# A Mamba layer before attention and experts: x_proj in two 64-column tiles, delta in two row groups, chunk ends in four 32-column tiles, carries on VectorE

## The reference, cut to what matters

```python
dbc = einsum('ble,re->blr', xb, xp_w)              # 512 channels -> 48 rows
delta, Bm, Cm = dbc[..., :16], dbc[..., 16:32], dbc[..., 32:]
delta = softplus(einsum('blr,er->ble', delta, dtw) + dtb)   # rank 16 -> 512 channels
dA = exp(delta[..., None] * -exp(a_log))           # 512 channels x 16 states
mi = delta[..., None] * Bm[:, :, None, :] * xb[..., None]
def scan_fn(carry, inp):
    h, v = carry
    dA_t, mi_t, C_t = inp
    v = 0.6 * v + mi_t                             # fixed decay
    h = dA_t * h + v                               # decay from the data
    return (h, v), einsum('ben,bn->be', h, C_t)
```

## Time and profile before

| | |
|---|---|
| median of three runs | 1678.77 us |
| the profiled execution: its own time | 1679.95 us |
| its span, first to last instruction | 1678.4 us |
| TensorE busy | 1533.2 us (91%) |
| VectorE busy | 1188.1 us (71%) |
| GpSimd busy | 1002.5 us (60%) |
| ScalarE busy | 826.3 us (49%) |

### The profile page before, as it was taken

One profiled execution on the slowest core, in us unless ns is written; L12 is line 12 of the kernel. 1 busy time (PEld: TensorE's weight loads), 2 busy tenths in 40 slices (PEclk: granted clock), 3 DMA queues, 4 the chain that ended last, 5 costly groups with the idle time before them and its releaser, 6 DMA issues.

```text
span 1678.4 us, 23940 instructions
## 1 busy us (share of the span) xinstructions
PE 1533.2 (91%) x8930; PEld 1159.4 (69%) x8930; DVE 1188.1 (71%) x1910; ACT 826.3 (49%) x1175; POOL 1002.5 (60%) x820
## 2 busy tenths in 40 slices
PE   4689999999999999999999997858979898899997
PEld 2468878978978978978879897623434443476776
DVE  3389979879879879879879879447666672433344
ACT  3756556656656656556556543203545556411110
POOL 1469778978978969969969987653111100024441
PEclk9899999999999999999999999968999999999999
DMA  4100100101100100100101120146141400612124
GB/s 139 42 26 27 51 26 27 51 26 52 51 26 27 51 26 27 51 26 27 51 26 41 74 87 14 36 91 138 22 92 21 81 1 1 258 38 64 63 67 166
DMA packets 38113, 92.78 MB, mean 55 GB/s; under 512 B 9136, under 2 KB 21936, under 8 KB 33520
## 3 DMA queue, kind: packets, MB, share of 16 engines
q1 hardware_dynamic: 29392, 73.68, 13.9%
q0 software_dynamic: 7584, 16.53, 3.8%
q10 hardware_dynamic: 1024, 1.05, 0.3%
HBM read 64.88 MB, written 9.57 MB: 44 GB/s over the span
## 4 chain that ended last, share of the span: by engine, by line
PE 76%; DVE 13%; issue 4%; ACT 3%; POOL 1%; SPq 1%; DMA 1%; DVEq 0%; ACTq 0%; POOLq 0%
PE psum L483 23%; PE psum L464 10%; PE psum L420 5%; PE psum L1495 4%; PE psum L1480 4%; DVE uw L512 4%; DVE hst L606 4%; PE psum L1064 4%; PE psum L1046 2%; PE psum L444 2%; PE psum L455 2%; PE psum L1030 2%; PE psum L426 2%; PE psum L434 2%; ACT pT L1119 2%
## 5 line engine op out<-in xcount | busy, mean ns | idle before, releaser
L774 POOL TENSOR_TENSOR hst<-hst,cb 128x512 f32<-128x512 f32 x399 | 512.8, 1308 | 136.1 <-DVE hst L606 135.0
L606 DVE TENSOR_TENSOR_SCAN hst<-dA,hst,psum 128x256 f32<-128x256 f32 x399 | 277.0, 729 | 84.5 <-PE psum L483 82.3
L606 DVE TENSOR_TENSOR_SCAN hst<-dA,psum 128x256 f32<-128x256 f32 x399 | 252.8, 668 | 38.8 <-ACT dA L716 19.7
L483 PE MATMUL psum<-filt,uT 128*128 128x172 f32 (+1 forms) x1536 | 267.9, 311 | 10.7 <-DVE hst L606 9.1
L483 PE MATMUL psum<-filt,c_early 128*128 128x172 f32 (+1 forms) x1536 | 268.1, 311 | 7.9 <-DVE hst L606 5.6
L483 PEld LDWEIGHTS psum<-filt,c_early 128*128 128x128 f32 x1536 | 235.2, 192 | 47.6 <-issue 27.3
L483 PEld LDWEIGHTS psum<-filt,uT 128*128 128x128 f32 x1536 | 233.5, 191 | 40.9 <-issue 19.8
L716 ACT ACTIVATE dA<-delta,alog 128x512 f32<-128x512 f32 x256 | 176.9, 721 | 150.3 <-DVE hst L606 120.2
L464 PE MATMUL psum<-ident,hst 128*128 128x128 f32 x1596 | 240.3, 274 | 0.7 <-POOL hst L774 0.6
L716 ACT ACTIVATE dA<-xres,alog 128x512 f32<-128x512 f32 x256 | 177.1, 720 | 123.5 <-DVE hst L606 97.4
L1191 DVE TENSOR_REDUCE nmax<-psum 128x2 f32<-128x1024 f32 x128 | 154.8, 1221 | 82.9 <-PE psum L1030 82.6
(11 more groups left out here) (213 smaller groups left out, 2346.3 us busy)
## 6 DMA issues: line engine op xcount, KB each, us to landing
cb<-c_rows SPq DMA_DIRECT2D x32, 1024.0 KB, 4.7
qk<-part SPq DMA_DIRECT2D x120, 64.0 KB, 2.4
qk<-part POOLq DMA_DIRECT2D x72, 64.0 KB, 4.5
w_up<-up_dram SPq DMA_DIRECT2D x8, 512.0 KB, 7.8
w_down<-down_dram SPq DMA_DIRECT2D x8, 512.0 KB, 14.3
w_up<-y_choice SPq DMA_DIRECT2D x8, 512.0 KB, 8.1
xm<-x_dram SPq DMA_DIRECT2D x4, 512.0 KB, 10.0
w_early<-w_in_dram SPq DMA_DIRECT2D x2, 1024.0 KB, 5.8
```

The source lines that it names most:

```text
L483: m = pe.matmul(bk[:, :, t0:t0 + width], uT[k % 2][:, c, et * P:(et + 1) * P], filt[:, f % 2, c, n2:n2 + 2, 0:width], start=True, stop=True)
L606: dve.tensor_tensor_scan(h[:, t0:t0 + HS], dA[:, st % NDA, t0:t0 + HS], bank("v", i)[:, n * HS:(n + 1) * HS], h[:, t0 - 1:t0] if t0 else 0 ...
L774: pool.tensor_tensor(h, h, cb[:, q % 2, state_of(i)[1] % GN, :], ALU.mult).then_inc(g_done, 1)
```

## The change

- **x_proj**: the weights' 48 rows become 64 (delta, B, delta again, C) and the 512 tokens two halves of 256. Each half goes to its own 64-column tile of the array: output partitions 0 to 63 and 64 to 127 of one bank, 256 columns each. ScalarE takes them out with two copies of 64 x 256 in place of one of 128 x 512.
- **delta**: contraction over 32 rows (16 of them zero weights) in place of 128; even `d` pieces use rows 0 to 31, odd ones rows 32 to 63. In the plan `d` 0 and 1 both stand at step 23, `d` 2 and 3 at step 25.
- **dbcT** transposes 32 rows in place of 48.
- **bend / bcol** (VectorE): the two `bend` multiplications now read `dbcT` from PSUM and stand ahead of `bcol`, which frees the bank; before they read `bcol` from SBUF behind it. `bend` has 32 columns per chunk in place of 128, and zeros in the rows of the starting state.
- **chunk ends**: no `c` waits for another. Chunks 0 to 3 go to four 32-column tiles of one bank, chunk 4 to another bank; both pieces stand at step 53. ScalarE's copies stand at step 54 (four) and 55 (one); each waits for both pieces.
- **carries** (new, VectorE): four `scalar_tensor_tensor` of 16 x 512, `uT[j+1] += 0.6**width * uT[j]` for j = 1 to 4, at steps 56 to 59. The first v matmul of a pass waits for the last of them.

```diff
-                    put(23 + m, "pe", "d", m)
+                    put(23 + m // 2 * 2, "pe", "d", m)
...
-                for c in range(NCH - 1):
-                    put(52 + 2 * c, "pe", "c", c)
-                    put(53 + 2 * c, "act", "c", c)
+                for q in range(2):
+                    put(53, "pe", "c", q)
+                for c in range(NCH - 1):
+                    put(54 + c // NQ, "act", "c", c)
+                for c in range(1, NCH - 1):
+                    put(55 + c, "dve", "carry", c)
...
                     for kt in range(ET):
-                        i = pe.matmul(bk, w_xp[:, l, kt, :], xbs[:, par, kt, NSTATE:NSTATE + S], start=kt == 0, stop=kt == ET - 1)
+                        for h in range(2):
+                            i = pe.matmul(bk[XP_ROWS * h:XP_ROWS * (h + 1), 0:HS], w_xp[:, l, kt, :],
+                                          xbs[:, par, kt, NSTATE + h * HS:NSTATE + (h + 1) * HS],
+                                          start=kt == 0, stop=kt == ET - 1, tile_position=(0, XP_ROWS * h))
...
-                    i = pe.matmul(bk, w_dt[:, l, j * P:(j + 1) * P], dbc[:, NSTATE:NSTATE + S], start=True, stop=True)
+                    r0 = j % 2 * BC
+                    i = pe.matmul(bk, w_dt[r0:r0 + BC, l, j * P:(j + 1) * P], dbc[r0:r0 + BC, NSTATE:NSTATE + S], start=True, stop=True,
+                                  tile_position=(r0, 0))
...
-                    pe.wait_ge(bank_act, emptied_by("act", k, "c", j - 1) if j else emptied_by("act", k, "u", NCH - 1))
-                    i = pe.matmul(bk, bend[:, j, :], uT[par][:, j, :], start=True, stop=True)
+                    pe.wait_ge(bank_act, emptied_by("act", k, "u", NCH - 1))
+                    w = P // NQ
+                    for c in range(j * NQ, min(j * NQ + NQ, NCH - 1)):
+                        p0 = c % NQ * w
+                        i = pe.matmul(bk[p0:p0 + w, :], bend[:, c, :], uT[par][:, c, :], start=True, stop=True, tile_position=(0, p0))
...
+                    dve.tensor_scalar(ends[:, :, 0:HCH - 1], starts[:, :, 0:HCH - 1], keep[:, 1:2], None, ALU.mult)
+                    dve.tensor_scalar(ends[:, :, HCH - 1], starts[:, :, HCH - 1], keep[:, 2:3], None, ALU.mult).then_inc(bend_done, 1)
                     dve.scalar_tensor_tensor(out=bcol[:, par], in0=tv[:, :, RANK:RANK + NSTATE], scalar=keep[:, 0:1], in1=carry_id[:].unsqueeze(1).to_broadcast([P, NCH, NSTATE]),
                                              op0=ALU.mult, op1=ALU.add).then_inc(bank_dve, 1)
...
+                elif what == "carry":
+                    if j < NQ - 1:
+                        dve.wait_ge(ends_out, (NQ - 1) * k + j + 1)
+                    else:
+                        dve.wait_ge(bank_act, emptied_by("act", k, "c", j // NQ))
+                    if j > 1:
+                        dve.wait_ge(carry_done, NQ * k + j - 1)
+                    to = uT[par][0:NSTATE, j + 1, :]
+                    dve.scalar_tensor_tensor(out=to, in0=uT[par][0:NSTATE, j, :], scalar=BETA ** CHUNKS[j][1], in1=to,
+                                             op0=ALU.mult, op1=ALU.add).then_inc(carry_done, 1)
...
-                    act.copy(dbc[:, NSTATE:NSTATE + S], bank(k, "xp", 0)).then_inc(bank_act, 1)
+                    act.copy(dbc[:, NSTATE:NSTATE + HS], bank(k, "xp", 0)[0:XP_ROWS, 0:HS])
+                    act.copy(dbc[:, NSTATE + HS:NSTATE + S], bank(k, "xp", 0)[XP_ROWS:2 * XP_ROWS, 0:HS]).then_inc(bank_act, 1)
```

More of the change, by code:

```diff
@@ L27 @@
 RANK = 16
-RBC = RANK + 2 * NSTATE
+BC = RANK + NSTATE
+C_ROW = 2 * RANK + NSTATE
+XP_ROWS = C_ROW + NSTATE
 L = 2
@@ L261, in plan_first @@
                     put("act", "u", c)
+                for q in range(2):
+                    put("pe", "c", q)
+                s += 1
                 for c in range(NCH - 1):
-                    s += 1
-                    put("pe", "c", c)
-                    s += 1
                     put("act", "c", c)
+                for c in range(1, NCH - 1):
+                    put("dve", "carry", c)
             def plan_front(k, at, start):
@@ L519, in dve_side @@
                         dve.wait_ge(filt_done, NG * (k - 1))
-                    tv = bank(k, "dbcT", 0)[:, 0:NCH * RBC].rearrange("p (j r) -> p j r", r=RBC)
+                    tv = bank(k, "dbcT", 0)[:, 0:NCH * BC].rearrange("p (j r) -> p j r", r=BC)
+                    ends = bend[:, :, 0:NSTATE].rearrange("p (h c) n -> p h c n", h=2)
+                    starts = tv[:, :, RANK:RANK + NSTATE].rearrange("p (h c) n -> p h c n", h=2)
+                    dve.tensor_scalar(ends[:, :, 0:HCH - 1], starts[:, :, 0:HCH - 1], keep[:, 1:2], None, ALU.mult)
+                    dve.tensor_scalar(ends[:, :, HCH - 1], starts[:, :, HCH - 1], keep[:, 2:3], None, ALU.mult).then_inc(bend_done, 1)
                     dve.scalar_tensor_tensor(out=bcol[:, par], in0=tv[:, :, RANK:RANK + NSTATE], scalar=keep[:, 0:1], in1=carry_id[:].unsqueeze(1).to_broadcast([P, NCH, NSTATE]),
                                              op0=ALU.mult, op1=ALU.add).then_inc(bank_dve, 1)
-                    dve.wait_ge(bank_dve, emptied_by("dve", k, "dbcT", 0))
-                    ends = bend[:, :, 0:NSTATE].rearrange("p (h c) n -> p h c n", h=2)
-                    starts = bcol[:, par].rearrange("p (h c) n -> p h c n", h=2)
-                    wide, last = CHUNKS[0][1], CHUNKS[HCH - 1][1]
-                    dve.tensor_scalar(ends[:, :, 0:HCH - 1], starts[:, :, 0:HCH - 1], toep[:, wide - 1:wide], None, ALU.mult)
-                    dve.tensor_scalar(ends[:, :, HCH - 1], starts[:, :, HCH - 1], toep[:, last - 1:last], None, ALU.mult).then_inc(bend_done, 1)
+                elif what == "carry":
[8 more added lines that the diff above has]
+                                             op0=ALU.mult, op1=ALU.add).then_inc(carry_done, 1)
                 elif what == "clip":
@@ L700, in act_side @@
                 elif what == "c":
-                    act.wait_ge(bank_full, filled(k, "c", j))
-                    act.copy(uT[par][0:NSTATE, j + 1, :], bank(k, "c", j)[0:NSTATE, :]).then_inc(bank_act, 1)
+                    act.wait_ge(bank_full, filled(k, "c", 1))
+                    p0 = j % NQ * (P // NQ)
+                    act.copy(uT[par][0:NSTATE, j + 1, :], bank(k, "c", j // NQ)[p0:p0 + NSTATE, :]).then_inc(
+                        bank_act if j in (NQ - 1, NCH - 2) else ends_out, 1)
                 elif what == "x_roots":
```

30 lines of the change are left out of this document (17 added, 13 removed).

## The result

The changed kernel takes 1683.19 us (1677.56 to 1689.35, median of 20 runs) against 1677.68 us (1672.12 to 1682.26, 20 runs) for the one before: ratio 1.0031, interval 1.0020 to 1.0043. It is slightly slower, by 0.3%. The forecast of 1671.5 us was 11.7 us too low, and on the other side of no change. The change itself was missed by 12.8 us: 7.3 faster was forecast from a median before of 1678.77, and 5.5 slower was measured against 1677.68.

What follows compares the result with a forecast made beforehand. TensorE sets the pace, VectorE the end from step 3 to 8. 1679.95 - 6.5 (front) - 7 x (1.57 + 0.64) (x_proj, delta) + 14.2 (carries) = 1672.2; with the median 1.2 lower, forecast 1671.5 us, range 1651 to 1686.

Steps and rivals of the forecast that it cites:

- TensorE sets the pace, but from v 52 to v 9 VectorE does: Mamba loop: TensorE busy 131.13 of 132.00 us; VectorE sets the end around steps 3 to 8 of a pass.
- x_proj: Step 20, seven times: column tiles run side by side, 1.86 us for 3.43, 1.57 us saved each.
- delta: Steps 23 and 25: pairs of 1.0 us for 1.73; a wait for bcol leaves 0.64 us saved per pass.
- Carries: Steps 56 to 59: four VectorE instructions, some waiting for GpSimd's running one, take 5.5 us; 1.95 us lost per pass.
- The 1.95 is carried to step 9 and into the pass: Steps 3 to 9: order as before and VectorE bound, so the 1.95 us loss reaches the pass.
- Steady passes: x_proj and delta save, carries lose 1.95 us: a pass takes about 123.8 us for 124.06.
- Pass 0's front: Start of pass 0, up to the first scan: 6.5 us saved, 4 to 8, first scan at about 66.6.
- Each carry meets GpSimd in full & d saves nothing: Slower rival: carries cost 1.5 us more a transition and the delta pairs save nothing; 1685 us, chance 0.08.
- the clock rival: TensorE's clock falls in new waits at steps 62, 63 and 0, costing 23 us; 1695 us, chance 0.10.
- Tiles in turn: x_proj's tiles save nothing and the five c hold VectorE 2.4 us longer; 1699 us, chance 0.03.
- Half rate: Carries run at half throughput, 0.5 us more each, 2 a transition; 1685 us, chance 0.02.
- Carries are cheap: Carries don't wait for GpSimd, 0.7 us each, 2.8 in all; 1652 us, chance 0.12.

Runs made afterwards that it cites:

- nocarry: The changed kernel with the four carries left out, the first v of a pass waiting for the last copy: 1650.83 us, ratio .9834, pass 120.9 us.
- nox: The changed kernel with x_proj on one 64-column tile over all 512 tokens and one copy: 1697.02 us, ratio 1.0114, pass 127.0 us.
- twice_sbuf: psum53 plus four more scalar_tensor_tensor with both operands in SBUF, into a tile nobody reads: 1710.08 us, ratio 1.0203.
- second profile: The changed kernel run again without any edit: profiled total 1684.74 us, median 1683.73 us, ratio 1.0025.
- psum53: The changed kernel with carries reading the chunk end from PSUM, all four behind step 53's scans, ScalarE copying only the first end: 1657.68 us, ratio .9874.

## Why the prediction was wrong, step by step

- **TensorE sets the pace, but from v 52 to v 9 VectorE does: right with the carries.** Without them (nocarry) all that TensorE saves there is gained. The carries alone make VectorE the bound.
- **x_proj: right in kind, a little mis-sized.** 1.55 saved in its own bracket where 1.57 was forecast, but 0.19 goes in the pieces around it: 1.36. nox shows by itself that the tiles run side by side (1.70 against one tile after the other).
- **delta: mis-sized.** 0.64 was forecast, 0.24 measured. The wait for `bcol` came where it was put, 0.54 us instead of 0.9. What was missing is the way into and out of a tiled piece, 0.09 ahead of it and 0.10 behind. A pair costs 1.25 in all (0.09 + 1.06 + 0.10), not 1.0. Of the 0.40 missing here, 0.10 belongs to `xp`, whose longer v 21 falls into this stretch.
- **Carries: the failed step.** "Carries 1 and 2 each meet a running multiplication (1.8 each)": the walk was right up to the first carry (8.21 us behind step 53's v; 8.3 forecast), and the sum of the four was 6.6 instead of 5.5. The mechanism had the wrong reach. The first carry waited for the running multiplication and for two more that were ready when it came, and took 3.29; in twice_sbuf, with three more ready, the first took 5.06. Carries 2 and 4 met a running one alone (1.33, 1.32), and carry 3 none, for want of more ready work. The prediction had taken its rule from the maxima, which do wait for the running instruction alone, and a carry is not treated as they are. Of the 1.1 us more, 0.67 shows in the stretch (2.62 lost for 1.95); the walk's 0.3 for small waits and the air behind took the rest, which I did not follow further.
- **"The 1.95 is carried to step 9 and into the pass": too little.** Another 0.3 goes at step 11, where `bo` waits for GpSimd's gate, which ran 0.8 us later (and 0.09 ahead of `xp`). The prediction looked at GpSimd's sum (14% idle) and not at what it owes there.
- **Steady passes:** -2.21 + 1.95 = 123.8 forecast, -1.79 + 2.62 + 0.40 = 125.3 measured. Five of them are 7.5 of the 12.8 us by which the change was missed.
- **Pass 0's front: right in itself, mis-sized at the end.** 7.1 us at the first scan for 6.5, but 2.6 to 5.0 by the next `xp`: TensorE works there at a granted clock of 0.86 to 0.93 (before 0.96), so part of what is saved goes again. The forecast let all 6.5 reach the end. A shorter front does not by itself bring the lower clock: nocarry has 0.96 from 65 to 110 with its first scan at 67.66. What does was not tried.
- **The sum by stretches**, change against the kernel before, in us:

| | forecast | first profile | second profile |
|---|---|---|---|
| start to `xp` in pass 0 | -6.5 | -5.1 | -2.6 |
| to `xp` in pass 1 | +1.2 | -1.3 | +1.3 |
| five steady passes | -1.3 | +6.2 | +6.2 |
| rest | -1.2 | -1.1 | -0.3 |
| all | -7.8 | -1.2 | +4.6 |

The largest error stands in the steady passes. In the second row the forecast paid 5.5 us for the carries; they took 4.0 (0.67, 1.33, 0.65, 1.33).
- **The rivals.** "Each carry meets GpSimd in full & d saves nothing", 1685 us at a chance of 0.08, is nearest to what happened in time. In kind it is half right, and the closeness is partly luck: the carries took 6.6 us and not the 7.0 it means, the `d` save a little, and pass 0 gives back less than the forecast that it started from. Clock at steady passes 1.00: the clock rival is out. Tiles in turn: out by nox. Half rate: 0.65 us for 512 elements in carry 3 (0.7 was the forecast's full rate), out. "Carries are cheap" became true as a mechanism in psum53, not in this kernel.

## What to carry to other kernels

A VectorE instruction with both inputs in SBUF, put beside a GpSimd that has ready work, can cost far more than its own length: here the rest of the running instruction at least, and for the 16-partition carries everything that was ready when they came. Do not carry the price over from another kind of instruction; take one operand from PSUM where it already lies there, and drop the copy with it. In a ring of banks look up for each moved piece which piece stands a ring's length ahead: a wait that is moved away from one piece goes to the next, and may hide in its duration. An engine with 14% idle over the pass can still be the last one at one step. Price a tiled piece with the pieces on both sides of it, not by its own bracket.

## What the hardware showed that was not expected

- A 16x512 `scalar_tensor_tensor` with both inputs in SBUF takes 0.65 to 0.68 us alone, 3.29 beside one running and two ready GpSimd instructions, and 5.06 beside one running and three ready; with a PSUM operand 0.68 in the same place.
- A 128x512 `tensor_tensor` with both inputs in SBUF gets in after the running GpSimd instruction (1.59 us), though the next had been ready for 3 us; that one then takes 1.71 for 1.27.
- A float32 piece on one row group of 32 costs 1.06 us to the next start where the full array takes 0.86, and the pieces around it 0.19 more. Two such pieces on two row groups take the same 1.06 together, and the lateness of the second one's bank on top (1.41 and 1.55 for 0.36 and 0.50 us).
- Two 64-column tiles side by side take 1.88 us for x_proj, one tile after the other 3.58, the full array 3.43.
